# Attention and feed-forward on one core: softmax maxima and low parts over 1024 keys per instruction, one PSUM pair for the scores, and the value bias added to the normalised context

## What is computed

```python
def _L0_attn_ref(x, attn_qkvw, attn_qkvb, attn_ow, attn_ob):
    qkv = x @ attn_qkvw + attn_qkvb
    ...
    scores = jnp.einsum('bhqd,bhkd->bhqk', q, k) * scale
    probs = jax.nn.softmax(scores, axis=-1)
    ctx = jnp.einsum('bhqk,bhkd->bhqd', probs, v)
    ctx = jnp.transpose(ctx, (0, 2, 1, 3)).reshape(B, S, H)
    return ctx @ attn_ow + attn_ob
...
x = x + _L0_attn_ref(_layernorm(x, axis=-1), ...)
x = x + _L0_ffn_ref(_layernorm(x, axis=-1), ...)   # silu(x Wg) * (x Wu) Wd
```

## Time and profile before

| | |
|---|---|
| median of 3 runs | 3513.61 us (3511.58 to 3518.63) |
| the profiled execution: device time | 3510.52 us |
| its span, first to last instruction | 3508.6 us |
| busy share of the span | PE 94%, weight loads 73%, DVE 59%, ACT 41%, GpSimd 23% |
| mean granted PE clock | 0.964 of 2.4 GHz |
| chain that ended last | PE 73%, DVE 15%, DMA 4%, SP's issue 3% |

### The profile page before, as it was taken

How to read it: one execution, slowest core, us unless ns; L and a number is a source line. 1 busy time by engine, 2 the same in 40 slices (tenths; PEclk the granted TensorE clock), 3 DMA queues, 4 the chain that set the end, 5 groups by cost and what they waited for, 6 DMA issues and landing times.

```text
span 3508.6 us, 40890 instructions
## 1 busy us (share of the span) xinstructions
PE 3311.1 (94%) x15264; PEld 2552.3 (73%) x15264; DVE 2069.4 (59%) x3236; ACT 1453.7 (41%) x2702; POOL 808.5 (23%) x600
## 2 busy tenths in 40 slices
PE   6999999987989999999998999999879899999999
PEld 5676777654778888888676767677548788888885
DVE  5688888889552332332458888888894423223222
ACT  1478777777321111111015787777772211111110
POOL 1133333236400110110102333332463011010110
PEclk9999999998999999999789999999999999999996
DMA  3423343344311111111224233333443111111111
GB/s 105 122 76 95 87 106 87 87 119 125 133 43 54 54 36 53 55 37 37 99 78 112 76 109 82 92 91 87 119 133 112 43 60 48 36 60 48 37 45 48
DMA packets 110518, 274.62 MB, mean 78 GB/s; under 512 B 28720, under 2 KB 29872, under 8 KB 106224
## 3 DMA queue, kind: packets, MB, share of 16 engines
q1 hardware_dynamic: 110320, 272.02, 26.3%
HBM read 195.37 MB, written 76.02 MB: 77 GB/s over the span
## 4 chain that ended last, share of the span: by engine, by line
PE 73%; DVE 15%; DMA 4%; SPq 3%; ACT 2%; issue 1%; POOL 1%; POOLq 0%; ACTq 0%; DVEq 0%
PE ps L522 12%; PE ps L524 12%; PE ps L523 12%; PE ps L677 6%; PE ps L679 5%; PE ps L678 5%; PE ps L587 5%; PE ps L623 4%; PE ps L606 4%; PE ps L618 4%; DVE mx L890 4%; DVE pl L914 4%; SPq L1053 3%; DVE wl L848 2%; DMA wraw<-in_wqkv 1%
## 5 line engine op out<-in xcount | busy, mean ns | idle before, releaser
L890 DVE TENSOR_REDUCE mx<-ps 128x1 f32<-128x512 f32 x1024 | 696.0, 686 | 128.9 <-PE ps L587 117.3
L735 ACT ACTIVATE pu<-ps 128x512 f32<-128x512 f32 x1024 | 620.0, 605 | 346.3 <-PE ps L606 341.6
L1012 POOL TENSOR_TENSOR pl<-pu,ph 128x512 fp32r<-128x512 f32 x320 | 435.4, 1361 | 922.2 <-ACT ph L736 922.1
L736 ACT ACTIVATE ph<-ps 128x512 fp32r<-128x512 f32 x1024 | 620.0, 605 | 0.0
L914 DVE TENSOR_TENSOR pl<-pu,ph 128x512 fp32r<-128x512 f32 x704 | 550.3, 783 | 65.3 <-ACT ph L736 61.8
L522 PE MATMUL ps<-xh,gh 128*128 128x512 f32 x1376 | 546.0, 397 | 14.0 <-DVE gl L959 7.4
L524 PE MATMUL ps<-xl,gh 128*128 128x512 f32 x1376 | 541.9, 394 | 0.0
L523 PE MATMUL ps<-xh,gl 128*128 128x512 f32 x1376 | 538.1, 391 | 0.0
L587 PE MATMUL ps<-kst,qst 96*128 96x512 f32 x1024 | 432.4, 422 | 78.9 <-DVE mx L890 54.3
L968 DVE TENSOR_TENSOR hf<-ps,sg 128x512 f32<-128x512 f32 (+1 forms) x88 | 60.9, 692 | 721.4 <-PE ps L524 703.5
L606 PE MATMUL ps<-qst,kst 98*128 98x512 f32 x1024 | 421.6, 412 | 5.8 <-ACT ph L736 5.3
(11 more groups left out here) (83 smaller groups left out, 4981.8 us busy)
## 6 DMA issues: line engine op xcount, KB each, us to landing
wraw<-in_wqkv SPq DMA_DIRECT2D x24, 1024.0 KB, 5.0
q_d<-stg SPq DMA_DIRECT2D x384, 64.0 KB, 1.7
k_d<-stg SPq DMA_DIRECT2D x384, 64.0 KB, 1.7
qst<-q_d SPq DMA_DIRECT2D x64, 384.0 KB, 3.8
kst<-k_d SPq DMA_DIRECT2D x64, 384.0 KB, 4.6
graw<-in_wg SPq DMA_DIRECT2D x44, 512.0 KB, 4.5
graw<-in_wu SPq DMA_DIRECT2D x42, 512.0 KB, 3.6
draw<-in_wd SPq DMA_DIRECT2D x42, 512.0 KB, 3.7
```

The source lines that it names most:

```text
L735: e.activation(pu[sl][:, :], bk[:, :], ACT.Exp, scale=SCALE).then_inc(s["a_p"], 1)
L736: e.activation(ph[sl][:, :], bk[:, :], ACT.Exp, scale=SCALE).then_inc(s["a_ph"], 1)
L890: e.reduce_max(mx[:, (b * HEADS + j) % 2, t, half:half + 1], ps[2 + bank_of[what, b, j, t, half]][:, :], AX.X).then_inc(s["v_mx"], 1)
```

## The change

- The scores for the maxima go into one PSUM tensor of 1024 columns (`a_ps`, two banks). Step `a` is now a pair: PE writes both halves, one behind the other, and DVE takes one maximum over 1024 keys straight into `mm`. PE may write the next pair when that maximum has ended. Step `mm` and the tile `mx` are gone, and the transposed maxima use the same PSUM tensor.
- `pu`, `ph` and `pl` hold 1024 queries (NPU = 3 buffers of a pair). The exponentials stay at 512. Step `pl` is one subtraction over 1024, when both halves are there; 5 of 16 pairs are GpSimd's.
- The loop runs over pairs; in a pair's first unit stand the low part of the pair before and the scores of the pair 11 ahead.
- Step `vb`, `vtmp` and the tile of the value bias with its load are gone. ACT and DVE make the value parts straight from PSUM, and the bank is free when the low part has ended. Since the softmax weights sum to one, the bias is added to the normalised context: in ACT's high part (L753 before) as the activation's bias, in DVE's low part (L935 before) as a scalar operand.

```diff
-NPU = 5
+NPU = 3
...
-                groups.append(("vb", b, g, t))
-                defer(1, "vb", b, g, t)
+                groups.append(("vl", b, g, t))
+                defer(1, "vh", b, g, t)
...
-        def scores(j, t, half):
-            step("a", b, j, t, half)
-            if t == TT - 1 and half == 1:
-                step("mm", b, j)
+        def scores(j, t):
+            step("a", b, j, t)
+            if t == TT - 1:
                 defer(2, "mrow", b, j)
...
-        for i in range(2 * AHEAD):
-            scores(i // 16, i // 2 % TT, i % 2)
+        for i in range(AHEAD):
+            scores(i // TT, i % TT)
             due()
-            while spent < LEAD + PACE * (i + 1):
+            due()
+            while spent < LEAD + PACE * 2 * (i + 1):
...
+        for w in range(HEADS * TT):
+            j, t = w // TT, w % TT
+            if t == 0:
...
+            for half in range(2):
+                u = 2 * w + half
...
+                step("p", b, j, t, half)
+                if half == 0:
+                    if w:
+                        step("pl", b, (w - 1) // TT, (w - 1) % TT)
+                        pend += [((w - 1) // TT, (w - 1) % TT, h) for h in range(2)]
+                    if w + AHEAD < HEADS * TT:
+                        scores((w + AHEAD) // TT, (w + AHEAD) % TT)
+                due()
+                if len(pend) > 2:
+                    context(*pend.pop(0))
+                fill((u + 1) / 2)
+        step("pl", b, HEADS - 1, TT - 1)
+        pend += [(HEADS - 1, TT - 1, h) for h in range(2)]
...
-        ps = [ctx.enter_context(nc.psum_tensor(f"ps{i}", [P, 512], f32)) for i in range(8)]
+        st_ps, a_ps, pv_ps, bg_ps = (ctx.enter_context(nc.psum_tensor(f"ps_{n}", [P, 1024], f32)) for n in ("st", "a", "pv", "bg"))
+        ps = [pair[:, 512 * i:512 * i + 512] for pair in (st_ps, a_ps, pv_ps, bg_ps) for i in range(2)]
...
-        pu = [at(f"pu{i}", 72 + 4 * i, [P, 512]) for i in range(NPU)]
-        pl = [at(f"pl{i}", 72 + 4 * i, [P, 512], f32r) for i in range(NPU)]
-        ph = [at(f"ph{i}", 74 + 4 * i, [P, 512], f32r) for i in range(NPU)]
...
+        pu = [at(f"pu{i}", 72 + 8 * i, [P, S]) for i in range(NPU)]
+        pl = [at(f"pl{i}", 72 + 8 * i, [P, S], f32r) for i in range(NPU)]
+        ph = [at(f"ph{i}", 76 + 8 * i, [P, S], f32r) for i in range(NPU)]
...
-                        pe.wait_ge(*freed.get(nb, ("v_v", 0)))
-                        freed[nb] = ("v_v", of_v(b, g, t))
+                        pe.wait_ge(*freed.get(nb, ("v_vl", 0)))
+                        freed[nb] = ("v_vl", of_v(b, g, t))
...
-                    pe.wait_ge(*a_free[n])
-                    a_free[n] = ("v_mx", of_tile(b, j, t, half))
-                    e.matmul(ps[2 + n][:, :], qst[hd % 3][0:96, tile_of(t)], kst[hd % 3][0:96, halves(half)],
-                             start=True, stop=True).then_inc(s["p_a"], 1)
+                    pe.wait_ge(*a_free)
+                    a_free = ("v_mx", of_pair(b, j, t))
+                    for half in range(2):
+                        i = e.matmul(a_ps[:, halves(half)], qst[hd % 3][0:96, tile_of(t)], kst[hd % 3][0:96, halves(half)],
+                                     start=True, stop=True)
+                    i.then_inc(s["p_a"], 1)
...
-                    pe.wait_ge("v_mm", of_head(b, j))
-                    pe.wait_ge(*a_free[n])
-                    a_free[n] = ("v_ml", of_head(b, j))
-                    e.transpose(ps[2 + n][0:TT, 0:P], mm[:, (b * HEADS + j) % 2, :], idt[:, :]).then_inc(s["p_m"], 1)
+                    pe.wait_ge("v_mx", of_pair(b, j, TT - 1))
+                    pe.wait_ge(*a_free)
+                    a_free = ("v_ml", of_head(b, j))
+                    e.transpose(a_ps[0:TT, 0:P], mm[:, (b * HEADS + j) % 2, :], idt[:, :]).then_inc(s["p_m"], 1)
...
+                    e.matmul(bk[0:65, :], vv, ph[sl][:, z], start=(t == 0), stop=False)
+                    if on_pool(m - 1):
+                        pe.wait_ge("g_pl", pool_lows(m))
                     else:
-                        pe.wait_ge("v_pl", n - pool_lows(n))
-                    e.matmul(bk[0:65, :], vv, pl[sl][:, :], start=False, stop=(t == TT - 1)).then_inc(s["p_pv"], 1)
+                        pe.wait_ge("v_pl", m - pool_lows(m))
+                    e.matmul(bk[0:65, :], vv, pl[sl][:, z], start=False, stop=(t == TT - 1)).then_inc(s["p_pv"], 1)
...
-                    act.wait_ge("v_v", n)
+                    act.wait_ge("p_v", n)
...
-                    src = vtmp[(n - 1) % 2][:, :].rearrange("p (h d) -> p h d", d=HD)
+                    src = ps[6 + bank_of[what, b, g, t]][:, 0:256].rearrange("p (h d) -> p h d", d=HD)
...
+                    act.wait_ge("p_pv", 2 * (m - NPU))
+                    e.activation(pu[sl][:, z], bk[:, :], ACT.Exp, scale=SCALE).then_inc(s["a_p"], 1)
+                    e.activation(ph[sl][:, z], bk[:, :], ACT.Exp, scale=SCALE).then_inc(s["a_ph"], 1)
...
-                    e.activation(xh[:, c, halves(half)], ca2[half][:, :], ACT.Copy).then_inc(s["a_ch"], 1)
+                    e.activation(xh[:, c, halves(half)], ca2[half][:, :], ACT.Identity,
+                                 bias=bqkv_c[:, 2 * KT + c:2 * KT + c + 1]).then_inc(s["a_ch"], 1)
...
-                elif what == "vb":
...
-                    e.tensor_tensor(vtmp[(n - 1) % 2][:, :], bk[:, 0:256], bv_b[:, 256 * g:256 * g + 256], ALU.add).then_inc(s["v_v"], 1)
...
-                    e.reduce_max(mx[:, (b * HEADS + j) % 2, t, half:half + 1], ps[2 + bank_of[what, b, j, t, half]][:, :], AX.X).then_inc(s["v_mx"], 1)
...
-                    e.reduce_max(mm[:, hd % 2, :], mx[:, hd % 2, :, :], AX.X).then_inc(s["v_mm"], 1)
+                    if t == 0:
+                        dve.wait_ge("p_m", hd - 1)
+                    e.reduce_max(mm[:, hd % 2, t:t + 1], a_ps[:, :], AX.X).then_inc(s["v_mx"], 1)
...
-                    j, t, half = at_
-                    n = of_tile(b, j, t, half)
+                    j, t = at_
+                    n = of_pair(b, j, t)
                     sl = (n - 1) % NPU
                     if not on_pool(n - 1):
-                        dve.wait_ge("a_ph", n)
+                        dve.wait_ge("a_ph", 2 * n)
                         e.tensor_tensor(pl[sl][:, :], pu[sl][:, :], ph[sl][:, :], ALU.subtract).then_inc(s["v_pl"], 1)
...
-                    e.tensor_tensor(xl[:, c, z], ca2[half][:, :], xh[:, c, z], ALU.subtract).then_inc(s["v_cl"], 1)
+                    e.scalar_tensor_tensor(xl[:, c, z], ca2[half][:, :], bqkv_c[:, 2 * KT + c:2 * KT + c + 1], xh[:, c, z],
+                                           ALU.add, ALU.subtract).then_inc(s["v_cl"], 1)
...
-            copy(bqk_c[:, :], bqk, "d_const")
-            copy(bv_b[:, :], bv.partition_broadcast(P), "d_const")
+            copy(bqkv_c[:, :], bqkv, "d_const")
```

129 lines of the change are left out of this document (42 added, 87 removed).

## The result

The changed kernel takes 3583.7 us (median of 4 runs, 3579.9 to 3588.7). The kernel before, run beside it, takes 3516.1 us (3511.6 to 3524.0). The ratio is 1.019, 95% interval 1.017 to 1.021: slower by 67.6 us. The profiled execution has a span of 3586.8 us and is the slowest of its four.

What follows compares the result with a forecast made beforehand. PE was taken to bound attention's long part, DVE to pace its last part. Terms of 29.5 us per batch, 59 for both, less 1 at the start, gave +58 and 3571 us; forecast case 3530 to 3605, overall range 3496 to 3616.

Steps and rivals of the forecast that it cites:

- one PSUM pair's loop: Attention: PE starts the next score pair only after the merged maximum ends; commonest pair's loop of 2.56 us has no slack.
- long part: About 600 us of each batch's attention, PE busy 97.5%; cheaper DVE work can win at most 28 us there.
- Heads' ends: Transposed maxima at each head's end wait for a maximum released half a pair earlier: 24 against about 8 us, +16 per batch.
- Other DVE instructions between two maxima: Attention: DVE's weight, q, k and value work and ScalarE's copies delay maxima: 19 against some 8 us, +11 per batch.
- Scores ahead: The 11 pairs of scores made ahead: a loop of 2.1 us against 1.87 us of products, +3 per batch.
- Last part: Attention's last 150 us per batch: DVE's 10 us less offset by DVE idling, 0, bounds -10 and +12.
- drain: After a batch's last score product: only the last pair's lo part, 0.53 us longer and unhidden, was priced, +1 per batch.
- Value bias: 64 additions leave DVE: -1.5 per batch (bounds -4 and +2); one load fewer at the start, -1 us.
- The feed-forward part: Between the two batches' attention: PE without gaps, claimed not touched by the change, no term in the sum.
- the last part did not decide: Faster rival: DVE's 10 us per batch come off whole in attention's last 150 us, 3490 us; chance 0.19.
- GpSimd's long instruction: Slower rival: GpSimd's lo part of about 2.4 us blocks DVE's next one, 26 us more per batch, 3623 us; chance 0.15.
- thin head's end: Head ending in a pair with 3 background products after its second exponential's product: transposition 1.25 us late, 12 times, 15 us.

Runs made afterwards that it cites:

- without heads' ends: Transposition of the maxima left out (output differs), in the changed kernel: 3528.3 us; in the kernel before with only the value bias edit: 3484.9 us.
- the changed kernel with padding and halves: Changed kernel plus an unused 128-byte-per-partition tensor, with GpSimd's lo parts in two instructions of 512 keys: 3554.4 us, ratio 1.012.
- the halves: GpSimd's lo parts in two instructions of 512: value bias, merged lo part, two score banks, 3519 to 3496.5 us; changed kernel with the padding, 3554.4 us.
- the kernel with the merged maximum: Kernel before with the value bias edit and the merged maximum on one PSUM pair, lo parts still of 512: 3553.0 us, ratio 1.011.
- the padding: Changed kernel plus one unused tensor of 128 bytes per partition where the table of half maxima stood: 3569.2 us, ratio 1.015.

## Why the prediction was right, and where it was not

The sign and the cause held: slower, because of one PSUM pair's loop with the long lo part in it. The total, 58 us forecast and 67.6 measured, comes near partly by luck: the long part's waits were priced at 54 us and the experiments give some 38 for these terms, of which a good part is clock that the sum didn't have, while some 35 us of other losses were priced at 2. Term by term, for both batches:

- **Heads' ends, +32 forecast, +30 measured** (55 less 25). Both sizes were too low by about the same amount, 24 and 8 per batch against 29.5 and 15.1 in the long part, so their difference came out right; that is luck as well. By PE's idle time alone the difference is 10 us per batch (19.1 less 9.2), and most of the rest is, by the estimate, the lower clock behind the longer waits, which the sum had no term for. The +4 that the scores ahead cost per batch belong here as well: they vanish with the transposition.
- **Other DVE instructions between two maxima, +22 forecast, 4 per batch measured** (601.6 to 605.8 without heads' ends). The step that was mis-sized is, as I read it, the moment at which a late maximum begins to cost. I let the load of the next score product start at 2.56 us; PE does p first, and the product behind it starts at 2.79, so 0.2 us of lateness per pair are free. (The sum's own terms put the lo part's start at 1.17 + 1.57 = 2.74 and not 2.77, 0.18 us into the next pair; 0.16 was measured.) I had also counted some 8 us of such waits as already there, and they are there still (17.4 and 14.4 us of waiting loads).
- **Scores ahead, +6 forecast, +7 measured, by another cause.** I priced the loop over each of the 11 pairs. The loop costs nothing; the one head's end among the 11 costs it all (29.0 against 25.2 us without the transposition).
- **Last part, 0 forecast; drain, +2.** Up to the last score product the two kernels differ by 6.5 and 3.8 us (124.6 to 131.1, 125.8 to 129.6), inside my bounds. In this stretch stand two waits that the kernel before doesn't have: PE waits 5.8 us in batch 1 and 5.3 in batch 2 for one lo part of GpSimd, 11.1 of the 12.1 us of L623 above. But the kernel before has one of 6.3 and of 5.3 us for the copies of the transposed maxima in their stead, and where the 6.5 and 3.8 us come from stays open. The drain is the term that failed: +5.8 / +5.5 us instead of +1. I priced only the last pair's lo part, as if nothing else hung on GpSimd there. But without score products ScalarE sets the pace (busy for 24.1 of the 27.0 us before), and in its queue, between the exponentials, stand the high parts of the divided contexts (`xh`, L754), which wait for GpSimd's division (`ca`, L1009). That division stands behind the 2.4 us lo parts. In the drain of after, and of the changed kernel with padding and halves:

```profile
ACT xh L754 <- POOL ca L1009: 6.5, 4, 2.5
PE ps_st L605 <- ACT ph L737: 5.4, 3, 3.2
```

```profile
PE ps_st L606 <- ACT ph L738: 3.5, 3, 1.7
ACT xh L755 <- POOL ca L1012: 3.1, 4, 0.9
```

  ScalarE has no such wait in batch 1's drain before, and 0.5 us in batch 2's. In the drains of all fourteen kernels it is 0 to 2.5 us with lo parts of 512 (26.5 to 29.7 us long), 5.1 to 8.2 us with GpSimd's lo parts of 1024 (31.9 to 36.1 us) and 2.4 to 4.8 us with them in halves (28.5 to 30.0 us). That GpSimd's instruction is the cause is shown by the halves, which give 4.2 us of the drain back; the granted clock, 0.80 in batch 1's drain after and 0.94 before, doesn't explain it, since a drain of 27.9 us has 0.84 (batch 2 of the kernel with the merged maximum).
- **Value bias, -3 and -1 at the start:** -3.5 by the ratio, with an interval from -8 to +1, so it isn't told from nothing.
- **The feed-forward part, "not touched": +14.5.** Missing from the sum altogether. No row of before could have shown it; that a diff which removes a tensor moves all that is allocated behind it was there to be seen.

These come to some 30 + 8 + 11 + 14.5 - 4, about 60 of the 67.6 us, and to 70 with the 10 us of the last part up to the last score product, with a few us of uncertainty in each.

The rivals: the last part did not decide (DVE's 10 us less did not show). GpSimd's long instruction costs time, but not where I put it: I gave it 26 us per batch in the long part, the halves took 5 off it, and PE's idle time there stayed. Its mechanism as I told it, blocking DVE's next lo part behind a weight's high part, isn't shown; the drain is where its cost can be read. The Trainium skill ("Perfetto Trace Analysis", Optimizing Scalar/DVE Operations) says of ScalarE and VectorE that, where they aren't saturated but make others idle, breaking up their instructions may let work be done sooner. The halves show the same for GpSimd: its lo parts in 320 instead of 160 instructions, 22.5 us less in one kernel and 15 in the other.

Of what was to be seen in the trace: the transposition's load waits 1.42 us at a thin head's end (1.2 forecast), the long part is 18 to 20 us longer (25 to 30), DVE 12 points less busy in it (5; I had compared work and not the stretched share as well), maximum 1220 ns and lo part 1301 (1.22 both). The load of the score product waits 14.4 us, not 50: the late maxima show at the transposition alone.

## What to carry to other kernels

Merging two instructions halves their count and also nearly doubles the time until the first result (DVE's maximum, 686 to 1220 ns); on an engine that isn't the bound only the second matters. Merge where nobody waits for the first half (DVE's lo part with two banks of scores behind it), and leave halves where a buffer or a waiting engine hangs on them (the maximum with one pair, GpSimd's lo part). A wait of one engine can reach the bound engine through a third one's queue, as GpSimd's lo part did through ScalarE's; look for it where the stage ends and few other instructions hide it. When a step is moved past a shared buffer, follow everything that must leave the buffer, not only what is waited for now. And when a tensor is removed, compare the pitch of matmuls in a part that the change doesn't touch before explaining the rest.

## What the runs showed of the hardware that I had not expected

With nothing waiting and a granted clock of 1.00, matmuls of 128x128 by 512 columns started every 0.2291 us or every 0.2319 us, depending on whether the buffers behind one small table lay 128 bytes higher in SBUF or not (1746 or 1725 in 400 us for the two kernels that differ by this alone; of the other twelve, those with the table or the padding have the shorter time). In the attention part, where the long part took 634.5 and 635.3 us with and without the padding, no such difference showed.
